# Summing nine dot products over 96 channels on Vector alone, without GpSimd's half sum

## The reference

```python
patches = _unfold(x, k).reshape(NL, c, k, k)
y = einsum('ncij,vc->nvij', patches, w_mask) / (x_norm * w_norm)
idx = argmax(y.reshape(NL, -1)); max_ch = idx // 9; max_col = idx % 9
sim_map_max = y[max_ch]                         # nine cosines with the chosen vector
integrate = max_act * max_sim + w_mask[max_ch] * (1 - max_sim)
inp = concatenate([integrate, sim_map_max])     # 96 + 9 values
h = leaky_relu(inp @ w_i1.T + b_i1); vcs = tanh(h @ w_i2.T + b_i2)
out = fold(conv(relu(vcs @ w_l1.T + b_l1) @ w_l2.T + b_l2))
x = x + out
x = x + ffn0(layer_norm(x)); x = x + lrn(layer_norm(x)); x = x + ffn1(layer_norm(x))
```

## Time and profile before

| what | us |
|---|---|
| median of three runs | 3559.07 |
| the profiled execution | 3554.84 |
| its span in the trace | 3553.0 |
| PE busy | 3011.0 (85%) |
| DVE busy | 2778.1 (78%) |
| ACT busy | 2832.7 (80%) |
| POOL busy | 2566.0 (72%) |

### The profile page before, as it was taken

How to read it: one execution, slowest core, us unless ns; L and a number is a source line. 1 busy time by engine, 2 the same in 40 slices (tenths; PEclk the granted TensorE clock), 3 DMA queues, 4 the chain that set the end, 5 groups by cost and what they waited for, 6 DMA issues and landing times. The chain is left out here.

```text
span 3553.0 us, 62660 instructions
## 1 busy us (share of the span) xinstructions
PE 3011.0 (85%) x18190; PEld 1688.2 (48%) x18190; DVE 2778.1 (78%) x10043; ACT 2832.7 (80%) x7303; POOL 2566.0 (72%) x3993
## 2 busy tenths in 40 slices
PE   5888888888888888888888888888888888888755
PEld 2444454454545445445544545454444555445432
DVE  6777888888888888888888888888888888888631
ACT  0444788888888888888888888888878888888977
POOL 2455787777778777777877777787777778777753
PEclk9999999999999999999999999999999999999855
DMA  3111121211112121111212111121212112121000
GB/s 88 38 45 47 45 63 52 65 54 57 61 57 62 52 67 51 57 61 56 62 52 67 52 58 60 57 62 52 66 51 64 55 57 62 52 66 42 24 31 35
DMA packets 64607, 195.78 MB, mean 55 GB/s; under 512 B 11394, under 2 KB 14732, under 8 KB 64268
## 3 DMA queue, kind: packets, MB, share of 16 engines
q1 hardware_dynamic: 54028, 172.89, 15.1%
q0 software_dynamic: 10240, 18.89, 2.1%
HBM read 134.72 MB, written 57.02 MB: 54 GB/s over the span
## 5 line engine op out<-in xcount | busy, mean ns | idle before, releaser
L527 ACT ACTIVATE ffn_hid<-banks 128x384 f16<-128x384 f32 x2304 | 1026.8, 487 | 260.0 <-PE banks L370 236.7
L393 PE MATMUL banks<-wcT,xc 128*128 128x512 f32 x2304 | 1187.8, 618 | 50.2 <-DVE mx L745 43.4
L745 DVE TENSOR_REDUCE mx<-banks 128x1 f32<-128x512 f32 x1152 | 781.4, 687 | 428.8 <-PE banks L393 427.6
L370 PE MATMUL banks<-ffn_xT,w1q 128*128 128x384 bf16 x2304 | 668.8, 343 | 177.3 <-ACT ffn_hid L527 138.0
L994 POOL TENSOR_TENSOR ffn_f<-ffn_y,b2q 128x864 f16<-128x864 f16 x256 | 465.3, 1818 | 288.3 <-DVE nb L731 209.7
L370 PEld LDWEIGHTS banks<-ffn_xT,w1q 128*128 128x128 bf16 x2304 | 226.1, 98 | 775.8 <-ACT ffn_hid L527 589.4
L393 PEld LDWEIGHTS banks<-wcT,xc 128*128 128x128 f32 x2304 | 414.5, 196 | 282.8 <-issue 140.8
L825 DVE TENSOR_SCALAR ffn_hid<-ffn_hid,b1q 128x1152 f16<-128x1152 f16 x768 | 405.8, 551 | 139.0 <-ACT ffn_hid L527 138.6
L996 POOL TENSOR_TENSOR x<-x,ffn_f 128x864 f32<-128x864 f32 x256 | 466.6, 1823 | 20.1
L560 ACT ACTIVATE ffn_x<-x,cols 128x96 fp8e5<-128x96 f32 x1152 | 461.3, 456 | 0.0
L560 ACT ACTIVATE ffn_x<-x,nb,roots 128x96 fp8e5<-128x96 f32 x1152 | 425.1, 456 | 0.0
(11 more groups left out here) (153 smaller groups left out, 4178.6 us busy)
## 6 DMA issues: line engine op xcount, KB each, us to landing
xt<-x_tok_in SPq DMA_DIRECT2D x128, 432.0 KB, 3.2
xc<-x_chan_in SPq DMA_DIRECT2D x128, 432.0 KB, 3.6
out_tok<-x SPq DMA_DIRECT2D x128, 432.0 KB
win<-x_tok_in,xrow POOLq DMA_INDIRECT x128, 2.6
wrow<-vector_table,vidx POOLq DMA_INDIRECT x128, 2.9
shift<-shift_in SPq DMA_DIRECT2D x1, 960.0 KB
vector_table<-wtab SPq DMA_DIRECT2D x1, 384.0 KB, 2.9
w1raw<-w_in SPq DMA_DIRECT2D x1, 288.0 KB
```

The costliest lines, as they stand in the source:

```text
L370: last = pe.matmul(bank[:, 0:GW], w1q[:, ffn.layer, c * P:(c + 1) * P], ffn.xT[:, g * GW:(g + 1) * GW], start=True, stop=True)
L393: last = pe.matmul(ps_score[score_bank(j)], xc[p][:, j, :], wcT[:, :], start=True, stop=True)
L527: return nc.scalar.activation(dst, src, ACT.Copy)
L745: nc.vector.tensor_reduce(mx[p][:, j:j + 1], ps_score[score_bank(j)], AX.X, ALU.max).then_inc(score_taken, 1)
```

## The change

GpSimd's second instruction of the dot products is left out, with its buffer and its semaphore, and the signal that the products are ready is given by the multiplication. DVE sums all 96 channels of `prod_dot`, where it summed the 48 of `half_dot`. All other instructions stay as they are and in their order.

```diff
-        half_dot = sb("half_dot", [P, J, C // 2])
...
-        dot_chain, prod_dot_ready, inp_ready = sem("dot_pool_chain"), sem("prod_dot_ready"), sem("inp_ready")
+        prod_dot_ready, inp_ready = sem("prod_dot_ready"), sem("inp_ready")
...
-                f3c.link(nc.vector.tensor_reduce(dots[:, :], half_dot[:, :, :], AX.X, ALU.add),
+                f3c.link(nc.vector.tensor_reduce(dots[:, :], prod_dot[:, :, :], AX.X, ALU.add),
...
-                tt(prod_dot[:, :, :], xt[:, f2 & XT - 1], unit, ALU.mult).then_inc(dot_chain, 1)
-                pool.wait_ge(dot_chain, f2 + 1)
-                tt(half_dot[:, :, :], prod_dot[:, :, 0:C // 2], prod_dot[:, :, C // 2:C],
-                   ALU.add).then_inc(prod_dot_ready, 1)
+                tt(prod_dot[:, :, :], xt[:, f2 & XT - 1], unit, ALU.mult).then_inc(prod_dot_ready, 1)
```

## The result

The changed kernel takes 3606.51 us (median of 4 runs, 3603.79 to 3610.56) against 3559.36 us: 47 us more, ratio 1.0135 with a 95% interval of 1.0117 to 1.0152. The forecast was 3599 us. The profiled execution has a span of 3604.3 us, 51.3 us above that of before. Lines up to the product carry a number one lower than before (L797 is the sum, L806 makes `inp`, L392 the scores, L409 the turn, L983 the product), those behind it in the file are four lower (L1013 was L1017). In the experiments, each one's own edit shifts the numbers again.

A forecast was written before the change was run, and what follows sets the result against it. No engine is full; the order of waits sets the pace, with PE bound by DVE behind the sum. 51.3 less 3 is +48, less 8 for the stall gives +40 us: 3599 us, range 3582 to 3620.

The forecast's parts named there:

- The sum's price: DVE's sum grows from 432 to 864 values, costing 0.45 us more per sum (ends 0.43 and 0.59).
- It passes in full in plain steps: PE's loads for inp and the first score wait on DVE, so 0.45 us passes on 114 times, 51.3 us.
- Late pixels take some back: Where PE's load waits for a gathered pixel, the delay is partly hidden: -3 us, at most 5.4.
- The column step's start hides the sum: In 14 column steps PE's backlog leaves slack of 0.45 and 0.73 us: cost 0, without this cover 6 us.
- The stall's end: In the column step's middle, DVE is no longer held by POOL's half sum: -8 us, bounds -12.6 and 0.
- 0.6 of 0.9 us: Saving taken per column step out of L708's stall by POOL's removed instruction; times 14, -8 us.
- 114 x 0.45: PE's 114 waits for inp, each lengthened by the longer sum's 0.45 us: 51.3 us.
- the clock as a rival for plain steps: PE's longer idling drops its clock in 84 plain steps, 0.5 us each, +42 us: 3641 us; chance 6%.
- the ring: The ring of waits between engines that makes a plain step's 24.86 us, with DVE's sum standing in it.

The follow-up runs named there:

- twice-made sum: The changed kernel with Vector's sum of 96 channels made twice in a row, first into a buffer nobody reads; 3810.12 us, ratio 1.0687.
- e2_sum_48: The changed kernel with Vector summing only the first 48 channels of the product, GpSimd's half sum still left out; 3541.53 us, ratio 0.9951.
- the fillers: Five unread matmuls per early ramp step ahead of PE's turn of inp; 3589.01 us on the changed kernel, 3546.21 us on the one before.
- e3_ramp_filled: The changed kernel with five unread matmuls on PE ahead of the turn of inp in the first steps; 3589.01 us, ratio 1.0085.

## Why the prediction was right

The forecast was +40 us; it came to +51.3 in the profiled execution and +47 in the medians, on the right side and within the range.

- **The sum's price.** Forecast 0.45 us, measured 0.97 - 0.51 = 0.46 at its place and 0.44 in the step. The difference of paces of two reductions was the right row to take; the durations gave 0.51 in the forecast.
- **It passes in full in plain steps.** Right: 25.31 us foretold, 25.30 measured, with the wait for `inp` at 0.97 us (0.9 foretold), 114 times, and POOL's wait at 2.18 us (2.1). The twice-made sum shows the same slope over a further 0.97 us wherever the clock stayed full.
- **Late pixels take some back.** 3 us foretold. 85 plain steps x 0.44 are 37.4 us and 31.6 were measured, so 5.8 us came back. Before, the plain steps took 5.7 us beyond their median in all, 2.9 of it in the 16 steps in which PE waited for a pixel; in the changed kernel nothing is left of either part. So 2.9 us are the late pixels, as foretold, and what made the other 2.8 is open. Waits for the pixel fell from 18.1 to 7.3 us over the span.
- **The column step's start hides the sum.** PE's load for `inp` there has no wait in the changed kernel either, and DVE's wait before the third maximum shrinks by 0.38 us. Here are PE's load and that maximum after, and the same maximum before:

```profile
2021.35 0.13 PEld L409 LDWEIGHTS banks<-ident,inp 128*106 128x106 f32 x1
```

```profile
2025.09 0.69 DVE L744 TENSOR_REDUCE mx<-banks 128x1 f32<-128x512 f32 x1 [0.92 <-PE banks L392]
```

```profile
1988.11 0.69 DVE L745 TENSOR_REDUCE mx<-banks 128x1 f32<-128x512 f32 x1 [1.30 <-PE banks L393]
```

- **The stall's end.** Forecast -8 us, measured -8.3 in the column steps. With 48 channels on Vector they gain 12.1 us (e2_sum_48), so the longer sum takes 3.9 us of it back, 0.28 in each. But my reason for taking 0.6 of 0.9 us was not what happened. I had POOL's product come 0.45 us later against DVE. It starts 0.12 us behind L873, as it did behind L874 before, because DVE is held by POOL's instructions ahead of it as well. L854 ends with L1013, and is held 0.17 us longer than its like before (the third row); L850 just ahead of it takes 0.37 us where L851 took 0.19:

```profile
2031.31 0.91 DVE L854 SCALAR_TENSOR_TENSOR lbuf<-lbuf 128x72 f32<-128x72 f32 x1
```

```profile
2031.30 0.83 POOL L1013 TENSOR_TENSOR x<-x,cols 128x384 f32<-128x384 f32 x1
```

```profile
1994.15 0.74 DVE L855 SCALAR_TENSOR_TENSOR lbuf<-lbuf 128x72 f32<-128x72 f32 x1
```

  So part of POOL's delay reaches DVE there after all (L873 comes 9.78 us behind the third maximum, L874 9.44 before), and the full stall of 0.85 us is saved later on. The size was right by luck: two errors cancel.
- **The term that was mis-sized** is the ramp, which I had counted as thirteen plain steps within 114 x 0.45: 5.9 us, and it is 21.4. I had the clock as a rival for plain steps, priced from the column step, and gave it 6 chances in 100, but never looked at the ramp's clock, 0.94 before. That rival says that no row shows a fall at a gap of 1 us; the ramp of the same trace shows them behind 0.81 us. Its price of 0.5 us for a fall was too low as well: a fall in a plain step of the twice-made sum cost 1.36 us. In the ramp PE has less work in a step (busy 263.9 of 316.8 us, where a plain step has 22.20 of 24.86). Its wait for `inp` just ahead of a fall of the clock, before and after:

```profile
208.10 0.32 PE L410 MATMUL banks<-ident,inp 128*106 128x128 f32 x1 [0.81 <-DVE inp L807]
```

```profile
219.36 0.32 PE L409 MATMUL banks<-ident,inp 128*106 128x128 f32 x1 [1.25 <-DVE inp L806]
```

  In the fourth to the ninth step of the ramp the wait is 0.81 us in every one before and 1.25 us in every one after. Before, the clock fell in every second of these steps; with the wait 0.44 us longer it fell in each. With the fillers PE waits not at all in the kernel before and 0.44 us in the changed one, and the clock stays full in these steps of both. Of the 15.5 us beyond the sums (21.4 - 5.9) the fillers take away 10.9.

Sum: 37.4 - 5.8 + 6.2 (window) - 8.3 + 21.4 + 0.4 = 51.3.

## What to carry to other kernels

Cheap work on an engine that is idle for part of the time may still be the right place for it: ask at which point of the ring the work would stand on the other engine, and count it in full if two waits hang on it within a few hundredths of a microsecond. Work that must be done on a busy engine costs little where that engine waits anyway; the same 0.97 us cost 0.46 net at the step's start and nothing in the usual step's wait of 1.17 us, until the gathered pixel set the pace. Before adding a delay to each step, read the granted clock in every kind of step, the lightly loaded ones of the ramp above all.

## What the runs showed of the hardware

- PE's clock fell to 1.2 GHz in steps in which it had waited for another engine: behind 2.82 us of waiting in the column step, behind 1.78 us in 66 of the 85 plain steps of the twice-made sum, and behind 0.81 to 1.25 us in the ramp, where it is less busy. The wait alone does not settle it: the other 19 plain steps of the twice-made sum had the same 1.78 us at full clock, and with a wait of 0.82 us the clock fell in none of the 85 plain steps of the changed kernel and in 5 of e3_ramp_filled. Sixty matmuls that nobody reads made the kernel before 0.5% faster (0.9952). The Trainium skill, TensorE: Matmul & The Clock Gate, Part 1, ties the grant to recent activity; the fillers agree, since they change nothing else.
- DVE is held to the end of a POOL instruction in the column step: L702 2.04 us instead of 0.18, L825 1.35 instead of 0.51, L854 0.91 instead of 0.23, each ending within 0.4 us of POOL's. The sum of 864 values, one input in SBUF, kept to 1037 to 1052 ns in all 128 cases; in the plain step shown it lies beside POOL's `moments`.
